# Two waits ahead of GpSimd's additions in a two-layer transformer kernel

## What is computed

```python
x = x + L0_attn(layernorm(x))   # 16 heads of 8; q and k scaled to length 1; softmax(g * q.k) @ v
x = x + L0_ffn(layernorm(x))    # best of 8 experts, hidden 32, gelu
x = x + L1_attn(layernorm(x))   # 16 heads of 64, causal softmax, output projection
x = x + L1_ffn(layernorm(x))    # two best of 8 experts, hidden 512, then a layer norm
```

## Time and profile before

| | |
|---|---|
| median of three runs | 1604.84 us (1592.28 to 1605.28) |
| profiled execution | 1582.83 us, span 1581.1 us |
| busy, share of the span | TensorE 84%, VectorE 62%, ScalarE 55%, GpSimd 38% |
| mean granted clock of TensorE | 0.948 of full speed |

### The profile page before, as it was taken

One profiled execution on the slowest core, in us unless ns is written; L12 is line 12 of the kernel. 1 busy time (PEld: TensorE's weight loads), 2 busy tenths in 40 slices (PEclk: granted clock), 3 DMA queues, 4 the chain that ended last, 5 costly groups with the idle time before them and its releaser, 6 DMA issues.

```text
span 1581.1 us, 28399 instructions
## 1 busy us (share of the span) xinstructions
PE 1330.5 (84%) x9302; PEld 798.6 (51%) x9302; DVE 980.0 (62%) x3308; ACT 861.7 (55%) x1679; POOL 603.8 (38%) x783
## 2 busy tenths in 40 slices
PE   4777898888888888888888888889888886889982
PEld 1233444454545444544454455445555554677872
DVE  3565565656676666666666666664565664566784
ACT  4766565556555655565556555645343453455563
POOL 1000332233243324332433243325344445357675
PEclk8879899999999999999999999999898998999997
DMA  8060890000000000000000000000101000123322
GB/s 312 1 236 1 9 3 1 1 8 8 1 15 8 8 1 15 8 8 1 15 8 8 1 14 1 8 1 14 54 8 74 8 8 19 43 82 94 112 80 87
DMA packets 65454, 54.67 MB, mean 35 GB/s; under 512 B 41016, under 2 KB 51648, under 8 KB 65056
## 3 DMA queue, kind: packets, MB, share of 16 engines
q1 hardware_dynamic: 60768, 43.48, 13.1%
q0 software_dynamic: 4544, 9.38, 1.7%
HBM read 21.03 MB, written 31.81 MB: 33 GB/s over the span
## 4 chain that ended last, share of the span: by engine, by line
PE 58%; DVE 20%; ACT 11%; issue 6%; POOL 2%; POOLq 1%; DMA 0%; SPq 0%; ACTq 0%; DVEq 0%
PE scores L1733 10%; PE work L1673 8%; PE outs L1879 7%; PE outs L1752 7%; DVE scores L1227 6%; ACT a_buf L937 6%; PE scores L1702 4%; PE work L1782 4%; DVE ra L1220 3%; ACT ra L943 3%; PE scores L1866 2%; DVE parts L1262 2%; PE outs L1958 2%; PE work L1765 2%; DVE a_buf L1196 2%
## 5 line engine op out<-in xcount | busy, mean ns | idle before, releaser
L1227 DVE CUSTOM_DVE_ANT_0 scores<-scores,mask_qk 128x512 f32<-128x512 f32 (+3 forms) x512 | 239.2, 519 | 200.2 <-PE scores L1702 199.1
L786 POOL TENSOR_SCALAR_AFFINE_SELECT big<-big 128x256 f32<-128x256 f32 x256 | 101.0, 407 | 553.1 <-ACT big L931 552.9
L937 ACT ACTIVATE a_buf<-scores 128x1024 f32<-128x1024 f32 x256 | 248.0, 1028 | 104.3 <-PE scores L1866 104.0
L931 ACT ACTIVATE big<-scores 128x1024 f32<-128x1024 f32 (+1 forms) x192 | 169.4, 883 | 202.8 <-PE scores L1733 200.8
L1733 PE MATMUL scores<-ra 64*128 64x512 f32 (+3 forms) x1536 | 186.8, 349 | 37.7 <-ACT a_buf L937 24.4
L796 POOL TENSOR_TENSOR big<-big 128x768 f32<-128x768 f32 x64 | 116.9, 1827 | 151.1 <-PE work L1765 150.8
L1733 PEld LDWEIGHTS scores<-ra 64*128 64x128 f32 x1536 | 122.7, 190 | 88.3 <-ACT big L931 29.7
L1752 PE MATMUL outs<-big 128*64 128x512 f32 (+3 forms) x1024 | 163.1, 447 | 0.0
L1879 PE MATMUL outs<-a_buf 128*16 128x512 f32 x1024 | 145.9, 645 | 1.5 <-ACT a_buf L937 1.4
L1012 ACT ACTIVATE big<-scores,b_sb 128x128 f32<-128x128 f32 x312 | 89.7, 370 | 75.7 <-PE scores L1946 75.6
L943 ACT CAST ra<-work 128x512 fp32r<-128x512 f32 x128 | 75.0, 586 | 96.5 <-PE work L1673 95.4
(11 more groups left out here) (223 smaller groups left out, 2644.5 us busy)
## 6 DMA issues: line engine op xcount, KB each, us to landing
sorted_rows<-xrows SPq DMA_DIRECT2D x34, 520.0 KB, 7.0
qkT<-sorted_rows SPq DMA_DIRECT2D x78, 65.0 KB, 1.9
a_buf<-in_w SPq DMA_DIRECT2D x2, 2048.0 KB, 7.5
a_buf<-in_x SPq DMA_DIRECT2D x8, 256.0 KB, 2.8
x_rows<-x SPq DMA_DIRECT2D x8, 256.0 KB, 2.0
ra<-x_rows SPq DMA_DIRECT2D x8, 256.0 KB
a_buf<-choice_rows SPq DMA_DIRECT2D x6, 256.0 KB, 4.0
yT<-choice_rows SPq DMA_DIRECT2D x5, 256.0 KB, 3.0
```

Of the source, the lines that this page charges most:

```text
L931: activation(prob1(g, i), d[:, :, 0:256] if i == 2 else d, ACT.Exp, scale=SCALE1).then_inc(unit_free("pair", g, i), 1)
L937: activation(prob0(c)[:, i * 1024:(i + 1) * 1024], unit_wait(act, "cosine", c, i), ACT.Exp).then_inc(unit_free("cosine", c, i), 1)
L1227: return v.tensor_tensor_reduce(scores_, scores_, mask_qk[:, SEQ - width:SEQ], -1.0, 3e38, ALU.add, ALU.min, neg_max[:, qt, j:j + 1])
```

## The change

`sum_blocks` gets p, s and h and waits for two more semaphores before its additions: in every step but the last for the maxima's parts of the next pair, and, in steps that have them, for the operands' low parts of the same step.

```diff
-            def sum_blocks(g):
+            def sum_blocks(g, p, s, h):
 
                 causal(g, 2, 0)
+                if g + 1 < ALL_PAIRS:
+                    pool.wait_ge(negmax_ready, g + 2)
+                if p in (1, 3, 5) and s is not None:
+                    pool.wait_ge(parts_ready, s * GROUPS0 + p // 2 + 2)
+                if p == 7 and h is not None:
+                    pool.wait_ge(parts_ready, h * GROUPS0 + 1)
                 if g:
                     work_wait(pool, "sum", g - 1)
                 pool.wait_ge(prob_masked, 4 * (g + 1))
...
-                    sum_blocks(o.g)
+                    sum_blocks(o.g, p, o.s, h)
```

## The result

The changed kernel took 1585.91 us in the median of 20 runs (1575.76 to 1597.92), the kernel before 1592.47 us (1589.86 to 1614.88, 20 runs). That ratio is of the means, 1586.49 and 1595.84 us; the medians alone give 0.9959. It is faster by 0.4 to 0.6%, which is less than the 1% of the forecast's own line, and by 6.6 us in the medians and 9.4 in the means, less than the forecast's 15.6 us.

What follows compares the result with a forecast made beforehand. TensorE's pauses were taken to bound the attention part, some from VectorE instructions stretched under GpSimd's additions. 8.3 + 5.8 + 1.5 = 15.6 us off 1604.8 gives 1589.2 us; overall range 1571 to 1605.

Steps and rivals of the forecast that it cites:

- p = 7, 8.3 us: Five p = 7 steps: low parts clear of the additions, TensorE's pause 2.16 to 0.51 us, 1.65 us saved each.
- Rival 1: p = 7 gain becomes a wait for ScalarE's exponentials, step 0 keeps its low clock: 1599 to 1604 us, chance 0.20.
- Step 0, 5.8 us: Additions held behind the maxima in step 0: 2.24 us less pause, plus 3.60 us from full clock; low end 2.2.
- Step 62, 1.5 us: Second maxima instruction in step 62 takes 0.20 instead of 1.71 us, TensorE's 2.00 us pause shrinks; low end 0.
- p = 1, 3: 0: Low parts' wait in p = 1 and 3: passed at once, except step 3, whose transpositions were not late; no gain.
- Step 45: 0: Step 45 (p = 5): the clash only moves from the low parts to VectorE's standardization of four rows; no gain.
- The passed waits, "passed at once": Maxima's wait in 61 steps, low parts' in 16: already fulfilled, semaphore reading covered by GpSimd's wait for the sums; no cost.
- The sum: Whole kernel: 8.3 + 5.8 + 1.5 = 15.6 us saved.
- The clock: Granted clock: full after step 0, worth 3.60 us; other gains or losses from low stretches were left to rivals.
- rivals 2 and 3: Clock's low stretches go, 1574 to 1584 us (chance 0.17), or new ones come, 1612 to 1625 us (0.08).
- rival 3: Pauses of 0.5 to 1.3 us in most steps come to be followed by low-clock stretches: 1612 to 1625 us, chance 0.08.
- the forecast's own sign: Refutation test: the prediction is wrong if the number of the clock's low stretches changes by more than two.

Runs made afterwards that it cites:

- the repeated comparison: The unedited changed kernel run again beside the kernel before and a version also waiting for standardized rows in p = 5: 0.9914 of before, -15.4 us at equal clock.
- the p = 7 wait alone: Changed kernel with only the wait for the operands' low parts in p = 7 kept: 0.9961 of the kernel before, -12.0 us at equal clock.
- the maxima's waits alone: Changed kernel with only the waits for the maxima's parts kept: 1.0008 of the kernel before, -5.3 us at equal clock.
- the passed waits alone: Changed kernel without the waits that hold additions back (steps 0, 62, 3, 45, all p = 7): 1.0061 of the kernel before.

## Why the prediction came out as it did

- *p = 7, 8.3 us.* Right in place and size: pause 2.16 to 0.50 us, and the next late thing was ScalarE's cast of the key, as said. Rival 1 (given back at the start of the next step) is refuted by the timeline of step 31.
- *Step 0, 5.8 us.* Right: 0.80 us of pause (0.76 forecast), no low stretch behind it, 6.28 us (6.31).
- *Step 62, 1.5 us.* Right: 2.00 - 0.49.
- *p = 1, 3: 0.* Right. *Step 45: 0.* The clash moved to the standardizations, 4.28 us; the pauses of 1.45 and 1.69 us became one of 3.21:

```profile
1048.74 4.28 DVE L1202 TENSOR_SCALAR a_buf<-res,mean,rstd 128x128 f32<-128x128 f32 x4
...
1054.27 0.75 PE L1858 MATMUL work<-ident_r,parts 128*128 128x128 f32 x4 [3.21 <-DVE ra L1226]
```

- *The passed waits, "passed at once".* Wrong in the premise that the wait for the sums covers what reading them takes, and so in the sign that the additions start 0.1 us behind the sums elsewhere. In step 37 the sums end at 892.60 (891.79 + 0.81) and the additions start 0.25 us later; in the kernel before it was 0.10 us (895.70 - 895.60). In steps with the maxima's wait alone it is 0.15 us. With 0.15 us more, two standardizations instead of one take their 0.34 us before the additions start, and the pause is 1.73 instead of 2.31 us. Step 37 before, then after:

```profile
894.79 0.81 PE L1765 MATMUL work<-big,ones 128*64 128x384 f32 x4
...
895.70 1.84 POOL L796 TENSOR_TENSOR big<-big 128x768 f32<-128x768 f32 x1 [2.62 <-PE work L1765]
```

```profile
891.79 0.81 PE L1771 MATMUL work<-big,ones 128*64 128x384 f32 x4
...
892.46 3.74 DVE L1202 TENSOR_SCALAR a_buf<-res,mean,rstd 128x128 f32<-128x128 f32 x4
892.85 1.91 POOL L802 TENSOR_TENSOR big<-big 128x768 f32<-128x768 f32 x1 [2.77 <-PE work L1771]
...
897.45 0.54 PE L1858 MATMUL work<-ident_r,parts 128*128 128x128 f32 x4 [1.73 <-DVE ra L1226]
```

  A gain of 5 x 0.58 = 2.9 us that the sum did not have.
- *The sum.* 15.6 us forecast, 15.4 at equal clock in the repeated comparison (the clocks of before in the first are not on record). That the two agree so closely is in part luck: with the 2.9 us it should have been 18.5, and this reading was 3.7 us above the pauses for the p = 7 wait alone and some 5 below them for the maxima's waits alone. That the parts do not add to the whole (12.0 + 5.3 = 17.3 alone, 15.4 together) stays within what it can tell.
- *The clock.* The term that was mis-sized. The forecast took 3.6 us of gain from it and left the rest to rivals 2 and 3, as two tails. The runs showed that it moves with every edit: mean clocks of 0.9318 to 0.9526 over the kernels here, some 12 us per 0.01. In the changed kernel new low stretches in p = 3 and p = 4 took the p = 7 gain back (rival 3's mechanism). Of the 15.6 us they left 6.6 in the medians and 9.4 in the means of the first comparison, and 12.6 in the means of the repetition; in the two profiles, 0.948 and 0.935, they took more than all of it. By the forecast's own sign it was wrong here: the low stretches of the whole trace went from 24 to 35, where more than two either way was to refute it. The forecast argued against rival 3 that step 31's 2.16 us keep the full clock. That held for the kernel before alone: nearly the same pause lost it where only waits in other steps were added.
- *The forecast's time*, 1589 us against 1585.91, is nearer than its gain by luck, because it set out from a median of three, 1604.84, and 20 runs of before have 1592.47. The gain from there was 6.6 us in medians, where 15.6 was said.

What stays open: why a low stretch begins where it does. The same pause is followed by one in one kernel and not in another, and the edits here moved this without a rule that the traces show. Open as well are the 3.7 us that the p = 7 wait alone gains over its pauses, and the 5 us that the maxima's waits alone lack.

## What to carry to other kernels

Here a GpSimd addition that reads SBUF while VectorE has two-input or standardizing work in SBUF stretched a VectorE instruction to about its own length (to 1.86 and 1.91 us, beside additions of 1.81 to 1.84), and the cost shows as a long maximum beside a normal median of VectorE's line. Look for it there, find which of these TensorE waits for, and put the additions behind *all* of them, the last in the queue too: here the change removed the first clash and left the next one, which was worth about twice as much in time and nearly as much in work. Where the whole moves by under 1%, list each execution with its granted clock and compare at equal clock as well, and read the pauses in the trace beside it; otherwise a right edit can look like a wrong one, as the maxima's waits did.

## What was not expected of the hardware

- A fulfilled wait is not free on GpSimd even while it is idle: the additions start 0.25 us behind the sums with two more waits, 0.15 us with one, 0.10 us with none, and this changed how many standardizations run before them.
- The granted clock moves with shifts of 0.05 to 0.15 us in the additions: 0.9318 with the passed waits alone, 0.9406 before beside it.
- With one pause per batch gone (p = 5), 0.0100 of mean clock came back, some 12 us along the slope, about as much as the 13.5 us of work that it saved.
- GpSimd's writes leave VectorE's two-input low parts alone (1.17 us for eight) and lengthen its standardizations a little (1.71 us for four instead of 1.12).
